# A perceiver block on one core: the batch loop of the second cross-attention written out on five engines

## The chip, the core and the metric

The kernel runs on one core of a Trainium2 chip. The time is in device microseconds (us), for one launch of the whole kernel. The core has five engines, each with an instruction stream of its own: TensorE (PE, with its weight loads shown apart as PEld), VectorE (DVE), ScalarE (ACT), GpSimd (POOL) and SyncE (SP), which here only issues transfers. They meet at semaphores.

## The reference, cut to what matters

The model has two layers. Each is a cross-attention to a context, a self-attention and a feed-forward part, on a state x of 8 x 64 tokens by 512. The change touches the cross-attention of layer 1:

```python
def _L1_xattn_ref(q, kv, key_padding_mask, Wq, bq, Wkv, bkv, Wo, bo):   # q 8x64x512, kv 8x1601x512
    Q = (q @ Wq + bq).reshape(Bc, Tq, H, HD).transpose(0, 2, 1, 3)       # H = 16 heads of HD = 32
    KV = (kv @ Wkv + bkv).reshape(Bc, Tk, 2, H, HD).transpose(2, 0, 3, 1, 4)
    attn = jnp.einsum('bhqd,bhkd->bhqk', Q, KV[0]) * scale
    attn = jnp.where(key_padding_mask[:, None, None, :], -jnp.inf, attn)
    out = jnp.einsum('bhqk,bhkd->bhqd', jax.nn.softmax(attn, axis=-1), KV[1])
    return out.transpose(0, 2, 1, 3).reshape(Bc, Tq, Dm) @ Wo + bo
```

Around it stand layer 0 (cross-attention, self-attention, a routed feed-forward part with 64 experts) before, and layer 1's self-attention and an 8-bit feed-forward product behind.

## The kernel before, in words

The kernel is written engine by engine, with the order of the work on each laid down by hand. The second cross-attention runs over batch elements b = 0 to 7 and, in each, over four units dc = 0 to 3 of four heads (128 feature columns). A unit does the following for its 1601 keys:

- PE turns the exponentials of the unit (L1085, `turn_p`: transposes, four groups tg = 0 to 3), multiplies them with the values (L1102, `pv`: matmuls on 32 columns of the array, the last group of which has 65 rows), and spreads the row sums (L1111, `sums`).
- Between these steps PE makes what the next units need. It is listed in `SLOTS`, a table of short words: "k2" is a key group (L1041, twelve matmuls on chunk 2 of the context), "v5" a value group (L1050, twelve matmuls on tile 5), "s1" the scores of one chunk (L1068, six matmuls). Key and value products use operands split in a rounded part and a rest, hence three matmuls for each of four slices. `SLOTS[0][0]`, with which every batch element opens, is "v0 k0".
- ACT makes the rounded keys `kh` (L1174), copies half of the turned exponentials to `pTx` (L1196), takes the exponentials (L1184), and rounds the context of b + 1 chunk by chunk in unit dc = 2 (L1167, `ctx_high`).
- DVE makes the keys' rest (L1238), adds the bias to the values (L1231), masks and takes maxima (L1249), copies the other half to `pTx`, and scales the result (L1301, L1303).
- POOL takes the next unit's queries (L987 to L992, `take_q`) and subtracts the rounded context from the raw one (L970, `ctx_rest`).
- SP loads the mask (L950) and four chunks of the context of the next batch element (L940, `load_ctx`), each behind a wait on PE's key groups, `kx_made`.

On each engine the batch elements are a hardware loop (`Fori`): PE, ACT and DVE loop over b = 0 to 6 and have b = 7 written out behind the loop; POOL has b = 0 ahead of its loop and loops over 1 to 7; SP has b = 1 ahead and loops over 2 to 7. In a loop b is a register, so every semaphore count that depends on b is worked out by the engine's sequencer, and slices by b are dynamic addresses (`bass.ds`). For PE:

```python
            for w in PRE[1]:
                token(-1, 3, w)
            with pe.Fori(0, B - 1) as b:
                for dc in range(4):
                    unit(b, dc)
            for dc in range(3):
                unit(B - 1, dc)
            unit(B - 1, 3, more=False)
```

PE's buffers of results are two banks of PSUM used in turn (`bank_of`), so PE waits for ACT's and DVE's reading of the group before the last; `kl_ready`, `vx_ready`, `ptx_act`, `ptx_dve` and `lo_ready` are the semaphores by which it would wait for the others.

Of the kernel before, what the change touches and what calls it, by code (L numbers as in the profile page):

```python
# [26 lines left out]
P = 128  # L27
B, S1, D, S2 = 8, 64, 512, 1601
# [25 lines left out]
def perceiver(nc, a, out):  # L54
# [3 lines left out]
    with ExitStack() as ctx:  # L58
        def sb(name, shape, dt=F32):
            return ctx.enter_context(nc.sbuf_tensor(name, shape, dt))  # L60

        def sem(name):
            return ctx.enter_context(nc.semaphore(name))
# [24 lines left out]
        mask8 = sb("mask8", [P, S2], U8)  # L88
# [176 lines left out]
        mask_ld = sem("mask_ld"); mask_set = sem("mask_set"); mask_part = sem("mask_part")  # L265
# [41 lines left out]
        def ln_pool(pool, n):  # L307

            pool.wait_ge(mv_ready, n + 1)
            nc.gpsimd.tensor_tensor(rstd[:, :], rstd[:, :], neg_half[:, :], ALU.pow).then_inc(rstd_ready, 1)  # L310
# [162 lines left out]
        def add_out_bias(pool, n, after):  # L473

            pool.wait_ge(xn_ready, NT * after)
            nc.gpsimd.tensor_tensor(x[:, :, :], x[:, :, :],
                                    bias_r[:, :].unsqueeze(1).to_broadcast([P, NT, D]), ALU.add).then_inc(xb_ready, 1)
# [457 lines left out]
        def xattn_sync(sp):  # L935
            def load_ctx(b, bv):

                for c, (k0, n) in enumerate(KC):
                    sp.wait_ge(kx_made, 4 * (4 * b - 1) + c + 1)
                    sp.dma_start(ctx_raw[c][:, :, 0:n],  # L940
                                 a["ctxT"][bv, :, :, k0:k0 + n].rearrange("e p c k -> (e p) c k")
                                 ).then_inc(ctx_ld[c], 16)

            sp.wait_ge(mask_set, 1)
            sp.dma_start(mask8[:, :], a["mask"][1:2, :].to_broadcast([P, S2])).then_inc(mask_ld, 16)
            load_ctx(1, slice(1, 2))
            with sp.Fori(2, B) as b:
                sp.wait_ge(ld_l1q, 16)
                sp.wait_ge(mask_set, b)
                sp.dma_start(mask8[:, :], a["mask"][bass.ds(b, 1), :].to_broadcast([P, S2])).then_inc(mask_ld, 16)  # L950
                load_ctx(b, bass.ds(b, 1))

            sp.wait_ge(vx_made, KT_N * 2 * B)
            for g in range(4):
                for odd in range(2):
                    r = slice(HD * (2 * odd + g // 2), HD * (2 * odd + g // 2 + 1))
                    sp.dma_start(slot[2][HD * g:HD * g + HD, odd::2, :], a["l1_wo"][r, g % 2::2, :]).then_inc(ld_l1o, 16)
            sp.dma_start(slot[3][:, :, :], a["l1a_wq"]).then_inc(ld_l1a, 16)
            sp.wait_ge(kx_made, 4 * 4 * B)
            sp.dma_start(slot[0][:, :, :], a["l1a_wk"]).then_inc(ld_l1a, 16)  # L960
            sp.dma_start(slot[1][:, :, :], a["l1a_wv"]).then_inc(ld_l1a, 16)
            sp.wait_ge(xb_ready, 3)
            sp.wait_ge(xx_ready, NT)
            sp.dma_start(bias_r[:, :], a["l1a_bo"].to_broadcast([P, D])).then_inc(ld_boa1, 16)
            sp.dma_start(slot[2][:, :, :], a["l1a_wo"]).then_inc(ld_l1ao, 16)
# [10 lines left out]
        def xattn_pool(pool):  # L976

            for v in (ctx_hi[3], ctx_lo[3]):
                nc.gpsimd.tensor_copy(v[:, :, KC[3][1]:], ident[:, P - (KW[3] - KC[3][1]):].unsqueeze(1)
                                      .to_broadcast([P, NC, KW[3] - KC[3][1]])).then_inc(pads_set, 1)  # L980
            nc.gpsimd.memset(qzero[:, :], 0.0).then_inc(pads_set, 1)
            ln_pool(pool, 3)

            def take_q(b, dc, bv):

                hi, lo = qb[dc % 2]
                nc.gpsimd.tensor_copy(qraw[:, :].unsqueeze(1) if not isinstance(bv, int) else qraw[:, :],  # L987
                                      qbd[:, dc, bv, :]).then_inc(q_taken, 1)
                pool.wait_ge(q_taken, 4 * b + dc + 1)
                nc.gpsimd.tensor_tensor(hi[:, :], qraw[:, :], qzero[:, :], ALU.add).then_inc(qh_set, 1)  # L990
                pool.wait_ge(qh_set, 4 * b + dc + 1)
                nc.gpsimd.tensor_tensor(lo[:, :], qraw[:, :], hi[:, :].bitcast(F32),  # L992
                                        ALU.subtract).then_inc(ql_ready, 1)
                pool.wait_ge(ql_ready, 4 * b + dc + 1)

            pool.wait_ge(pads_set, 3)
            pool.wait_ge(q_ready, 3 * NC)
            take_q(0, 0, 0)
            take_q(0, 1, 0)
            pool.wait_ge(ld_bo1, 16)  # L1000
            add_out_bias(pool, 2, 4)
            for dc in (2, 3):
                pool.wait_ge(sx_made, 8 * (dc - 1))
                take_q(0, dc, 0)
            with pool.Fori(1, B) as b:
                pool.wait_ge(q_ready, 3 * NC)
                pool.wait_ge(sx_made, 32 * b - 8)
                take_q(b, 0, bass.ds(b, 1))
                for c in range(4):
                    ctx_rest(b, c)  # L1010
                for dc in (1, 2, 3):
                    pool.wait_ge(sx_made, 32 * b + 8 * (dc - 1))
                    take_q(b, dc, bass.ds(b, 1))

        def xattn_pe(pe):
            def group(b, dc, w):
# [134 lines left out]
            pe.wait_ge(pads_set, 3)  # L1151
            for w in PRE[1]:
                token(-1, 3, w)
            with pe.Fori(0, B - 1) as b:
                for dc in range(4):
                    unit(b, dc)
            for dc in range(3):
# [11 lines left out]
        def xattn_act(act):  # L1169
            def key_high(b, dc, c):  # L1170
                h, n = key_half(b, dc), KN[c]
                act.wait_ge(kx_made, 4 * h + c + 1)
                f = (dc + 1) % 4
                nc.scalar.activation(kh[c % 2][0][:, 0:n], PS[:, bank_of(b, dc, ("k", c)), 0:n], ACT.Identity,  # L1174
                                     bias=bias_c[:, 3, f:f + 1]).then_inc(kh_ready, 1)

            def token(b, dc, w):
                if w[0] == "k":
                    key_high(b, dc, w[1])

            def ex(h, dc, p):
                act.wait_ge(sx_max, 2 * h + p + 1)
                v = sx[2 * (dc % 2) + p][:, 0:S2]
                nc.scalar.activation(v, v, ACT.Exp, scale=SC, bias=nmx[:, p:p + 1],  # L1184
                                     accum_out=rsx[:, p:p + 1]).then_inc(px_ready, 1)

            def unit(b, dc, more=True):
                u = 4 * b + dc
                share = SLOTS[dc] if more else [[]] * 5
                fetch = dc == 2 and not isinstance(b, int)  # L1190
                for w in share[0]:
                    token(b, dc, w)
                for tg in range(4):
                    n, w = (P, 4 * P) if tg < 3 else (rows(KT_N - 1), P)
                    act.wait_ge(ptx_made, 8 * u + 2 * tg + 1)
                    nc.scalar.copy(pTx[0][0:n, :, :].rearrange("p a b -> p (a b)")[:, 0:w],  # L1196
                                   PS[0:n, 2, 0:w]).then_inc(ptx_act, 1)
                    if fetch and tg in (0, 3):
                        ctx_high(b + 1, tg)
                    for w in share[tg + 1]:  # L1200
                        token(b, dc, w)
                    if fetch and tg in (0, 1):
                        ctx_high(b + 1, tg + 1)
                if more:
                    for p in range(2):
                        ex(u + 1, dc + 1, p)

            ctx_high(0, 2)
            ctx_high(0, 3)
            for w in PRE[0]:  # L1210
                token(-1, 3, w)
            xt_copy(act, nc.scalar.copy, 3, (0, 2))
            for w in PRE[1]:
                token(-1, 3, w)
            for p in range(2):
                ex(0, 0, p)
            with act.Fori(0, B - 1) as b:
                for dc in range(4):
                    unit(b, dc)
            for dc in range(3):  # L1220
                unit(B - 1, dc)
            unit(B - 1, 3, more=False)

        def xattn_dve(dve):
# [35 lines left out]
            def token(b, dc, w):  # L1260
                {"k": key_low, "v": v_out, "s": masked}[w[0]](b, dc, w[1])
# [67 lines left out]
            q_dve(dve, 2, 2, bank=0)  # L1329
            for w in PRE[1]:  # L1330
                token(-1, 3, w)
            with dve.Fori(0, B - 1) as b:
                for dc in range(4):
                    unit(b, dc)
            for dc in range(3):
# [445 lines left out]
```

## Time and profile before

| what | value |
|---|---|
| median of 3 runs | 1924.59 us (1922.11 to 1925.12) |
| the profiled execution | 1925.49 us, its span 1923.7 us |
| busy share of PE / DVE / ACT / POOL | 93% / 38% / 24% / 20% |
| mean granted clock of PE over the span | 0.955 |
| loop of the second cross-attention on PE | 894.13 to 1681.27 us |
| instruction packets: q8 / q14 | 101 (1.65 MB) / 45 (0.37 MB) |

The profile is of one execution. Start times in it are counted from the first instruction, and the span ends with the last. "Busy" is the time in which an engine has an instruction running; register, branch and semaphore instructions don't count. A wait named "issue" is one for which the profile shows no other engine as the cause. The granted clock of PE is a share of its full 2.4 GHz; 0.5 is 1.2 GHz.

### The profile page before, as it was taken

The numbers are of one execution on the slowest core, as the hardware profiler recorded it, in microseconds if no ns is written. First come the engines' busy times: TensorE is split into PE (matmuls) and PEld (weight loads), VectorE is DVE, ScalarE is ACT, GpSimd is POOL, SyncE is SP. The second block draws the span as 40 slices with busy tenths as digits, with TensorE's granted clock in tenths as the row PEclk, the third lists the DMA queues.
The fourth block names the chain that finished last, engine by engine and source line by source line (L and its number), as shares of the span: only waits on it lengthen the run. The fifth ranks groups of instructions, "written<-read, shape, count | busy, mean of one in ns | idle before, by whom it ended". The sixth has DMA issues, their size and how long they took to land. (4 is left out here: it accounts for less than half of the span.)

```text
span 1923.7 us, 33205 instructions
## 1 busy us (share of the span) xinstructions
PE 1781.9 (93%) x12620; PEld 1333.7 (69%) x12621; DVE 728.8 (38%) x1853; ACT 463.8 (24%) x720; POOL 383.7 (20%) x430
## 2 busy tenths in 40 slices
PE   8867899999999999969999999999999999998875
PEld 3545565666666666557888888888888888985453
DVE  2544561111111111144444545444444544443364
ACT  1111101222222222212422424232242413322010
POOL 2010004333333333311210303012030301200100
PEclk9788899999999999979999999999999999999987
DMA  7000229999999999820200202010020201002100
GB/s 274 0 1 1 105 86 323 333 333 329 333 335 330 332 334 333 256 86 1 61 16 2 70 7 70 7 51 26 2 70 7 70 7 48 23 1 88 49 1 22
DMA packets 67634, 231.88 MB, mean 121 GB/s; under 512 B 6880, under 2 KB 24544, under 8 KB 57376
## 3 DMA queue, kind: packets, MB, share of 16 engines
q1 hardware_dynamic: 53152, 196.29, 29.4%
q0 software_dynamic: 14336, 33.56, 7.2%
q8 instruction: 101, 1.65, 0.4%
q14 instruction: 45, 0.37, 0.1%
HBM read 208.07 MB, written 21.76 MB: 119 GB/s over the span
## 5 line engine op out<-in xcount | busy, mean ns | idle before, releaser
L1050 PE MATMUL PS<-S_r 128*128 128x256 f32 x2496 | 335.4, 290 | 20.0 <-issue 13.8
L1050 PEld LDWEIGHTS PS<-S_r 128*128 128x128 f32 x2496 | 310.8, 192 | 47.7 <-issue 39.3
L1041 PE MATMUL PS<-S_r 128*128 128x384 f32 (+1 forms) x1536 | 311.1, 352 | 0.0
L1041 PEld LDWEIGHTS PS<-S_r 128*128 128x128 f32 x1536 | 270.1, 190 | 10.8 <-issue 3.0
L1249 DVE CUSTOM_DVE_ANT_0 R<-PS,maskadd 128x384 f32<-128x384 f32 (+1 forms) x256 | 136.3, 570 | 30.3 <-PE PS L1068 27.9
L1587 DVE COPY R<-PS 128x256 f32<-128x256 f32 x64 | 27.2, 425 | 298.8 <-PE PS L1481 256.6
L1196 ACT COPY S<-PS 128x512 f32<-128x512 f32 (+1 forms) x128 | 64.4, 503 | 299.9 <-PE PS L1085 299.9
L987 POOL COPY S<-qbd 128x128 f32 (+1 forms) x32 | 9.4, 293 | 633.7 <-PE PS L1068 610.4
L1231 DVE TENSOR_TENSOR R<-PS,vbias 128x256 f32<-128x256 f32 (+1 forms) x208 | 88.2, 424 | 119.7 <-PE PS L1050 116.1
L970 POOL TENSOR_TENSOR S_r<-S,S_r 128x1536 fp32r<-128x1536 f32 (+2 forms) x32 | 118.4, 3720 | 70.4 <-ACT S_r L1167 70.4
L1492 PE MATMUL PS<-R 128*128 128x512 f32 (+1 forms) x288 | 131.6, 592 | 0.8 <-DVE R L1588 0.8
L1085 PE MATMUL PS<-ident,R 128*128 128x128 f32 (+1 forms) x832 | 117.8, 280 | 4.0 <-ACT R L1184 4.0
L1184 ACT ACTIVATE R<-R,nmx 128x1601 f32<-128x1601 f32 x64 | 104.0, 1628 | 63.0 <-DVE nmx L1257 63.0
L1421 POOL DMA_INDIRECT moe_acc<-x,scol x64 | 103.0, 1609 | 52.1 <-POOL scol L1417 48.3
L1545 ACT ACTIVATE x<-PS,w_tab 128x512 f32<-128x512 f32 x64 | 44.0, 688 | 287.1 <-PE PS L1492 287.1
L1291 DVE COPY S<-PS 128x512 f32<-128x512 f32 (+1 forms) x128 | 75.4, 589 | 74.9 <-PE PS L1085 74.2
L1085 PEld LDWEIGHTS PS<-ident,R 128*128 128x128 f32 (+1 forms) x832 | 90.8, 141 | 14.1 <-ACT R L1184 4.5
L1492 PEld LDWEIGHTS PS<-R 128*128 128x128 f32 (+1 forms) x288 | 54.7, 190 | 56.9 <-issue 45.9
L1238 DVE SCALAR_TENSOR_TENSOR kh0l<-PS,bias_c,kh0h 128x384 fp32r<-128x384 f32 x64 | 39.5, 618 | 133.9 <-ACT kh0h L1174 133.9
L1580 DVE TENSOR_TENSOR R<-R,PS 128x352 f32<-128x352 f32 x64 | 33.3, 521 | 143.8 <-issue 137.8
L1238 DVE SCALAR_TENSOR_TENSOR kh1l<-PS,bias_c,kh1h 128x384 fp32r<-128x384 f32 x64 | 41.7, 652 | 116.3 <-ACT kh1h L1174 116.3
L1470 PE MATMUL PS<-qbd,R 128*128 128x352 f32 x256 | 81.1, 459 | 0.7 <-ACT R L1527 0.7
(254 smaller groups left out, 2399.4 us busy)
## 6 DMA issues: line engine op xcount, KB each, us to landing
R<-in_w_gu SPq DMA_DIRECT2D x34, 1408.0 KB, 19.1
R<-in_w_dna SPq DMA_DIRECT2D x50, 512.0 KB, 17.6
qbd<-in_w_gu SPq DMA_DIRECT2D x16, 1408.0 KB
S<-in_w_gu SPq DMA_DIRECT2D x16, 1408.0 KB
S<-in_ctxT SPq DMA_DIRECT2D x24, 768.0 KB, 4.9
R<-in_w_dnb SPq DMA_DIRECT2D x50, 192.0 KB, 18.0
xnT<-in_w_dna SPq DMA_DIRECT2D x16, 512.0 KB
S<-in_ctxT SPq DMA_DIRECT2D x8, 898.0 KB, 5.0
```

What stands on the lines that cost most here:

```text
L970: nc.gpsimd.tensor_tensor(lo, raw, hi.bitcast(F32), ALU.subtract).then_inc(s, 1)
L1041: last = nc.tensor.matmul(PS[:, bank, 0:n], w3[0][:, cc, f0:f0 + P], x3[i][:, cc, 0:n], start=(cc == 0 and w3 is wkv_hi and x3 is ctx_hi), ...
L1050: last = nc.tensor.matmul(PS[:, bank, 0:256], x3[need][:, cc, k0:k0 + P], w3[1][:, cc, f0:f0 + 256], start=(cc == 0 and w3 is wkv_hi and x ...
L1085: last = nc.tensor.transpose(PS[0:n, 2 + p, i * P:(i + 1) * P], sx[2 * (dc % 2) + p][:, kt * P:kt * P + n], ident[:, :])
L1184: nc.scalar.activation(v, v, ACT.Exp, scale=SC, bias=nmx[:, p:p + 1], accum_out=rsx[:, p:p + 1]).then_inc(px_ready, 1)
L1231: nc.vector.tensor_tensor(vx[hf][0:n, i, :], PS[0:n, bank_of(b, dc, ("v", i)), 0:256], vbias[0:n, hf * 256:hf * 256 + 256], ALU.add).then_ ...
L1238: nc.vector.scalar_tensor_tensor(out=lo[:, 0:n], in0=PS[:, bank_of(b, dc, ("k", c)), 0:n], scalar=bias_c[:, 3, f:f + 1], in1=hi[:, 0:n].bi ...
L1249: nc.vector.tensor_tensor_reduce(out=sx[2 * ((dc + 1) % 2) + p][:, k0:k0 + n], in0=PS[:, p, 0:n], in1=maskadd[:, k0:k0 + n], scale=1.0, sc ...
L1291: nc.vector.tensor_copy(pTx[1][0:n, :, :].rearrange("p a b -> p (a b)")[:, 0:w], PS[0:n, 3, 0:w]).then_inc(ptx_dve, 1)
L1421: pool.indirect_dma_start(out=acc[k % 2], out_offset=bass.IndirectOffsetOnAxis(ap=scol[:, k:k + 1], axis=0), in_=yrow[k], in_offset=None, ...
L1470: last = nc.tensor.matmul(PS[:, gu, 0:I], xgT[k % 2][:, c, :], wgu[k][:, c, gu, :], start=(c == 0), stop=(c == NC - 1))
L1492: last = nc.tensor.matmul(PS[:, 3, :], hT[0:w, j, :], wdn[k][0:w, j, :], start=(j == 0), stop=(j == 2))
```

## The change

The `Fori` loops of the second cross-attention on the five engines become Python loops, so the code of every batch element stands in each engine's stream, one behind the other. The counts of the waits and the slices are then constants. Two conditions that told the loop's body from the rest by the type of b are put in another form and select the same work. The number and order of the computing and transferring instructions is the same on every engine. Each engine has no jump left in this stage: before, PE, ACT and DVE jumped back six times, POOL six times and SP five times. Two other loops, over expert tiles (`Fori` on SP and POOL and their like on the other engines), stay.

```diff
@@ xattn_sync
-            with sp.Fori(2, B) as b:
+            for b in range(2, B):
                 sp.wait_ge(ld_l1q, 16)
                 sp.wait_ge(mask_set, b)
-                sp.dma_start(mask8[:, :], a["mask"][bass.ds(b, 1), :].to_broadcast([P, S2])).then_inc(mask_ld, 16)
-                load_ctx(b, bass.ds(b, 1))
+                sp.dma_start(mask8[:, :], a["mask"][b:b + 1, :].to_broadcast([P, S2])).then_inc(mask_ld, 16)
+                load_ctx(b, slice(b, b + 1))
@@ xattn_pool
-            with pool.Fori(1, B) as b:
+            for b in range(1, B):
...
-                take_q(b, 0, bass.ds(b, 1))
+                take_q(b, 0, b)
...
-                    take_q(b, dc, bass.ds(b, 1))
+                    take_q(b, dc, b)
@@ xattn_pe
-            with pe.Fori(0, B - 1) as b:
+            for b in range(B - 1):
                 for dc in range(4):
                     unit(b, dc)
@@ xattn_act
-                fetch = dc == 2 and not isinstance(b, int)
+                fetch = dc == 2 and b < B - 1
...
-            with act.Fori(0, B - 1) as b:
+            for b in range(B - 1):
@@ xattn_dve
-            with dve.Fori(0, B - 1) as b:
+            for b in range(B - 1):
```

## Rows read from the trace of the kernel before

**Rows 1.** The page: busy time and share of the span.

```profile
PE 1781.9 (93%) x12620; PEld 1333.7 (69%) x12621; DVE 728.8 (38%) x1853; ACT 463.8 (24%) x720; POOL 383.7 (20%) x430
```

**Rows 2.** Windows: stretch, length, busy time of each engine, PE's clock, DMA share, GB/s.

```profile
894.13:1681.27 787.14, 770.99 (x7898) 686.94 (x7897) 367.28 (x1106) 253.31 (x364) 134.99 (x112) 0.99 0.11 33
...
1780.00:1923.70 143.70, 101.26 (x479) 60.08 (x480) 71.13 (x97) 17.27 (x30) 8.41 (x4) 0.81 0.07 24
```

**Rows 3.** All waits of PE from 894.13 to 1681.27: total, times, longest.

```profile
PE PS L1050 <- issue: 13.8, 6, 2.6
PE PS L1102 <- ACT S L1196: 2.4, 7, 0.5
```

**Rows 4.** Timeline of PE at the first jump back: start, length, group [wait].

```profile
999.97 0.32 PE L1102 MATMUL PS<-S,R 65*32 65x64 f32 x8
1002.51 2.38 PE L1050 MATMUL PS<-S_r 128*128 128x256 f32 x12 [2.23 <-issue]
1004.70 3.14 PE L1041 MATMUL PS<-S_r 128*128 128x384 f32 x12
1007.68 1.03 PE L1085 MATMUL PS<-ident,R 128*128 128x128 f32 x8
```

**Rows 5.** Timeline of PE where the seventh pass ends and b = 7 begins.

```profile
1677.40 0.32 PE L1102 MATMUL PS<-S,R 65*32 65x64 f32 x8
1677.65 1.70 PE L1050 MATMUL PS<-S_r 128*128 128x256 f32 x12
1679.18 2.25 PE L1041 MATMUL PS<-S_r 128*128 128x384 f32 x12
1681.27 1.04 PE L1085 MATMUL PS<-ident,R 128*128 128x128 f32 x8
```

**Rows 6.** Windows: L1102 (65x64) to the next L1085 at each pass's end.

```profile
999.97:1007.68 7.71, 5.48 (x34) 5.29 (x33) 1.22 (x4) 2.12 (x4) 0.00 (x0) 0.78 0.03 6
1113.32:1120.82 7.50, 5.46 (x33) 5.27 (x33) 1.22 (x4) 2.12 (x4) 0.00 (x0) 0.77 0.03 7
1226.62:1232.68 6.06, 3.95 (x33) 3.76 (x33) 1.22 (x4) 2.12 (x4) 0.00 (x0) 1.00 0.02 5
1338.27:1346.20 7.93, 5.49 (x33) 5.29 (x33) 1.22 (x4) 2.12 (x4) 0.00 (x0) 0.78 0.03 8
1451.79:1458.04 6.25, 3.92 (x33) 3.73 (x33) 1.22 (x4) 2.12 (x4) 0.00 (x0) 1.00 0.02 5
1563.86:1571.78 7.92, 5.30 (x33) 5.10 (x33) 1.22 (x4) 2.12 (x4) 0.00 (x0) 0.78 0.03 8
1677.40:1681.27 3.87, 3.87 (x34) 3.74 (x34) 1.22 (x4) 2.15 (x4) 0.00 (x0) 1.00 0.01 2
```

**Rows 7.** DMA queues, 1002.6 to 1010: packets, MB, share.

```profile
q8 instruction: 2, 0.03, 2.3%
```

**Rows 8.** Windows of units dc = 0 and 1: of b = 6 and of b = 7.

```profile
1571.78:1627.25 55.47, 55.47 (x565) 49.36 (x564) 25.81 (x77) 15.75 (x25) 2.44 (x6) 1.00 0.02 2
1681.27:1736.74 55.47, 55.47 (x566) 49.36 (x564) 25.54 (x77) 15.74 (x25) 1.22 (x3) 1.00 0.04 12
```

**Rows 9.** DMA queues: first 894.13 to 1681.27, then each stretch of rows 8.

```profile
q8 instruction: 76, 1.25, 0.7%
q14 instruction: 34, 0.28, 0.1%
...
q8 instruction: 4, 0.07, 0.5%
```

**Rows 10.** Timeline of ACT after the first jump and after the fall-through.

```profile
1007.88 0.58 ACT L1174 ACTIVATE kh0h<-PS,bias_c 128x384 fp32r<-128x384 f32 x1 [5.79 <-PE PS L1041]
...
1681.47 0.58 ACT L1174 ACTIVATE kh0h<-PS,bias_c 128x384 fp32r<-128x384 f32 x1 [1.92 <-PE PS L1041]
```

**Rows 11.** Timeline of SP: the context loads of b = 1 and of b = 2.

```profile
947.72 11.47 SPq L940 DMA_DIRECT2D S<-in_ctxT  x4
...
1061.43 11.46 SPq L940 DMA_DIRECT2D S<-in_ctxT  x4
```

## The prediction

> **What bounds the kernel now.** I read the page first, then went stage by stage. TensorE (PE) is busy for 93% of the span and VectorE, the next, for 38% [rows 1]. The page's chain of work that ended last is no help here: it reaches back only to 1780 us, after the loop. So the question is what PE does not do in the second cross-attention. That stage has a clean frame. Each unit opens with the same eight transposes of L1085; the first unit of the loop begins at 894.13 us, and the last batch element (b = 7), which is already written out behind the loop, at 1681.27 us. Between the two lie 787.14 us with PE busy for 770.99 of them [rows 2]. The view of waits says what fills the rest: 13.8 us in six waits put down to "issue", each before a group of L1050, up to 2.6 us long, and 2.4 us in seven short waits for ScalarE (ACT) [rows 3]. 770.99 + 13.8 + 2.4 = 787.2, so nothing else is missing. Nowhere in these 787 us does PE wait for VectorE (DVE), for GpSimd (POOL) or for a transfer.
>
> Six is the number of times a loop of seven passes jumps back. The timeline of PE shows the place. Unit dc = 3 ends with eight matmuls of L1102 of form 65x64, and the next pass opens with a value group of twelve matmuls of L1050, then a key group of twelve of L1041, then the transposes. At 999.97 us the eight start, 0.32 us long; the twelve start at 1002.51, after 2.23 us in which PE waits for nothing that the profile shows. They then take 2.38 us and the key group 3.14, and the transposes begin at 1007.68 [rows 4]. When the seventh pass ends, the same instructions follow, but in line, without a jump: the eight start at 1677.40, the twelve at 1677.65 with no wait, take 1.70 and 2.25 us, and the transposes begin at 1681.27 [rows 5]. The work is the same by the code (SLOTS[0][0] is "v0 k0" for every b) and by the counts in the windows (33 or 34 matmuls recorded). So the trace of before holds its own control: the price of a jump back is the length of this stretch with one, less 3.87 us.
>
> **The change part by part.** *The jumps of PE go.* The stretch from the eight matmuls to the transposes measures 7.71, 7.50, 6.06, 7.93, 6.25 and 7.92 us at the six jumps, and 3.87 at the fall-through [rows 6]. Less 3.87 each, that is 3.84 + 3.63 + 2.19 + 4.06 + 2.38 + 4.05 = 20.15 us. It splits in two: 13.8 us of waiting, and 20.15 - 13.8 = 6.4 us by which the matmuls behind the jump are slower. The slower ones are found at four of the six jumps, where PE is busy for 5.3 to 5.5 us in the stretch instead of 3.9, and there the mean granted clock is 0.77 or 0.78; at the other two it is 1.00 and the busy time 3.92 and 3.95, as in the fall-through [rows 6]. That is: after the idle gap the clock was granted at the lower of its levels (1.2 rather than 2.4 GHz) for a while, four times out of six, at 1.4 to 1.6 us each. With no gap, PE is busy without a break up to the key group, as at 1677, where the clock stayed at 1.00. I take all of it as gained: **-20.2 us**. The least it can be by these rows is the waits alone, -13.8, if the clock dips came from something other than the gap.
>
> What causes the 2.0 to 2.6 us is read from the instruction transfers. Two packets of the instruction queue q8, whose 16 KB blocks fit PE's number of instructions, run between 1002.6 and 1010 us, just behind the jump [rows 7]; the pace over the stretch is one in 787 / 76 = 10 us. The loop stretch has 76 packets of q8 with 1.25 MB [rows 9], some 16 KB each and eleven a pass: the body doesn't stay on the engine, it is brought in anew on every pass. A jump to its top finds nothing there. The Trainium skill ("Runtime: NRT & Kernel Launch", section "Instruction fetch mechanics") says that fetching ahead is purely sequential and that a taken branch to a place outside the small window stalls on the fetch of the target; by that rule all six waits go as well, and the trace agrees with its six waits of 2.0 to 2.6 us.
>
> *Written out, does the stream keep up?* The body of PE was fetched eleven blocks a pass already, so writing it out adds no traffic worth naming. Two units of b = 7, all in line, give the answer: 55.47 us with PE busy for 55.47 [rows 8] and four q8 packets. The same two units in the loop, from 1571.78, take 55.47 us too [rows 8], with four q8 packets as well [rows 9]. So blocks that follow in line cost nothing, and the register values that waits in the loop compare with, constants in b = 7, cost PE nothing either: that edit is worth **0.0 us** (bounds: none seen at 0.01 us in 55; over seven passes, below 0.2 either way).
>
> *ACT, DVE and POOL lose their jumps.* At PE's first jump ACT waits 5.79 us for PE's first key group; at the fall-through, without the gap, it still waits 1.92 us for PE [rows 10]. Their jumps lie under PE's work, so **0**. If that cover went, their own price would be at most the same 2.3 us a jump, and those are removed too, so this term cannot turn against the change. What the gap gave them was time to catch up. The fall-through shows that they don't need it: PE ran from 1681.27 for 55.47 us without a wait.
>
> *SyncE's loop.* It loads a mask and four context chunks for each b, and the four chunk loads hang behind waits on PE's key groups. In the first pass these are loads with a constant address, as they all will be afterwards; in the second the address comes from a register. Four issues span 11.47 us in the first pass and 11.46 in the second [rows 11]. No difference: **0**. Behind the loads stand ACT's rounded copies, then POOL's subtractions, then PE's groups of dc = 3 on the new chunks. PE shows no wait for POOL in any of the seven passes [rows 3], also not in the first, which it entered without a gap. The chain is released by PE's own key groups of dc = 2, later than the jump, so it moves with PE. If a chunk did come late, PE would wait at L1050 or L1041 for POOL, and the constant addresses would still not be its cause. No instruction is added to an engine, none changes its shape, and no new wait is made.
>
> *After the loop.* Everything from 1681 on starts 20.2 us earlier. From 1780 us to the end PE works in bursts and the mean clock is 0.81 [rows 2]. Where the dips fall may change a little; I allow two of them either way at 1.6 us, **0 +/- 3.2**.
>
> Sum: -20.2. The profiled execution took 1925.49 us for a span of 1923.7, so 1.8 us lie around it, and the median of the runs is 1924.59, 0.9 below it. The change comes off the span, so the forecast is 1924.6 - 20.2 = **1904.4 us**, 1.0% faster. The measurement can tell about 0.2% (3.9 us) from no change.
>
> **Rivals.** *1. Only the waits go.* The clock dips near the jumps have another cause, for instance they come due by themselves in a stage this dense. For it: dips came at only four of six jumps. Against it: the loop stage's mean clock is 0.99 [rows 2], and in b = 7 there is none at the same place. It gives 1924.6 - 13.8 = 1910.8 us. Chance 0.05.
>
> *2. The gap isn't the jump's.* Instruction blocks arrive late for some reason in the stream itself, and written-out code meets the same holes elsewhere. Then nothing is gained but the branch instructions: 1924.6 less under 1 us. The nearest evidence against it is rows 8: four blocks in line and no hole. The Trainium skill ("Advanced Engine Details and Errata", section "Control Flow Timing") gives about 108 ns for a compare-and-branch; by that figure alone six jumps would be 0.6 us, an estimate, and the change would be worth nothing. The rows at the jumps, 2.0 us and more, say otherwise. Chance 0.03.
>
> *3. Slower: the other engines starve.* ACT, DVE, POOL and SyncE bring their code over q14, 34 packets in the loop stretch [rows 9]. If in one long stream these came late, each exposed one would cost what PE's gap does, 13.8 / 6 = 2.3 us, since PE hangs on ACT and DVE within a unit for kh, kl and pTx. From 9 exposed of 34 on (9 x 2.3 = 20.7) it outweighs the gain; with half of them exposed, 17 x 2.3 - 20.2 = +18.9 us, 1943.5. Against it: in b = 7 these engines run in line and PE waits for none of them over 55 us. Chance 0.03.
>
> The forecast itself has 0.89. So faster by over 0.2%: 0.89 + 0.05 = 0.94; within 0.2%: 0.03; slower: 0.03. The range is the likeliest's own: 3.2 us for the clock on either side and about 1 for the median (the three runs spread from 1922.11 to 1925.12, more of it downward), which makes 1900 to 1908.6; I stretch the top to 1909.5, towards rival 1.
>
> **What the profile after would show.** PE's six waits before L1050 put down to "issue" are gone in the stage, and the twelve value matmuls start 0.25 us after the eight of L1102 at every b, as at 1677.65. The first jump lies between transposes at 894.13 and 1007.68 us, a pass of 113.55; the pass from 1571.78 to 1681.27, which ends in the fall-through, is 109.49 us. All seven should be 109.5 to 109.7 (113.55 - 3.84). The stretch from the first unit to b = 7 shrinks from 787.14 to 767.0 us. The instruction bytes of q8 stay near 1.65 MB. I would be wrong if PE showed "issue" waits of about 2 us at other places, if PE began to wait for kh, kl or pTx at more than the seven short places, or if the clock in the stage fell below 0.99.

## The result: 1902.8 us, and the profile after

The changed kernel took 1902.83 us in the median of five runs (1899.86 to 1904.58), the kernel before 1924.59 beside it. The ratio is 0.9888, with a 95% interval from 0.9873 to 0.9904. The forecast was 1904.4, in a range from 1900.0 to 1909.5.

The profiled span is 1900.6 us. PE's stretch from the first transposes of b = 0 to those of b = 7, which was 787.14 us [rows 2], is here, in the view of windows (stretch, length, busy time of PE, PEld, DVE, ACT, POOL, PE's clock, DMA share, GB/s):

```profile
891.46:1658.30 766.84, 764.72 (x7898) 681.04 (x7896) 364.94 (x1106) 253.24 (x364) 134.74 (x112) 1.00 0.11 33
...
1658.30:1713.77 55.47, 55.47 (x565) 49.36 (x564) 25.55 (x77) 15.72 (x25) 1.21 (x3) 1.00 0.05 12
...
1758.00:1900.60 142.60, 101.20 (x479) 60.10 (x480) 70.53 (x97) 17.25 (x30) 8.41 (x4) 0.81 0.06 23
```

It is 20.30 us shorter with the same 7898 matmul records, and two written-out units of b = 7 last the same 55.47 us as before [rows 8]. All waits of PE in the stretch (total, times, longest), against [rows 3]:

```profile
PE PS L1102 <- ACT S L1196: 2.1, 7, 0.5
```

The six waits of 13.8 us are gone and nothing came in their place. The timeline of PE where b = 1 begins, against [rows 4]:

```profile
997.16 0.32 PE L1102 MATMUL PS<-S,R 65*32 65x64 f32 x8
997.41 1.68 PE L1050 MATMUL PS<-S_r 128*128 128x256 f32 x12
998.93 2.28 PE L1041 MATMUL PS<-S_r 128*128 128x384 f32 x12
1001.05 1.03 PE L1085 MATMUL PS<-ident,R 128*128 128x128 f32 x8
```

It is 3.89 us from the eight matmuls to the transposes instead of 7.71; the fall-through before had 3.87. The instruction queues on the page, 101 and 45 packets before:

```profile
q8 instruction: 88, 1.44, 0.3%
q14 instruction: 26, 0.21, 0.0%
```

The other 2.8 us of the span's 23.1 are not the change's. The first transposes come 2.67 us earlier (894.13 to 891.46), and nothing ahead of them was changed. Over all runs below they come between 888.85 and 894.46 us, and kernels that keep PE's loop are found at both ends; so comparisons here go by the stretch, which leaves that scatter out. From the end of the stretch to the end of the span it is 242.3 us, and 242.4 before.

### The profile page after: what moved, and what is told of

The parts are those of the page before. It is cut to its first block and busy times, and to the rows that moved or that the text cites. A ratio compares the mean times of both kernels' runs of the same rounds, so it can differ in the third digit from the quotient of the medians.

```text
span 1900.6 us, 31650 instructions
## 1 busy us (share of the span) xinstructions
PE 1773.1 (93%) x12620; PEld 1325.8 (70%) x12621; DVE 726.5 (38%) x1853; ACT 463.4 (24%) x720; POOL 383.0 (20%) x430
## 3 DMA queue, kind: packets, MB, share of 16 engines
q8 instruction: 88, 1.44, 0.3%
## 5 line engine op out<-in xcount | busy, mean ns | idle before, releaser
L1050 PE MATMUL PS<-S_r 128*128 128x256 f32 x2496 | 331.2, 287 | 6.2 <-DVE kh0l L1238 6.2
L1050 PEld LDWEIGHTS PS<-S_r 128*128 128x128 f32 x2496 | 306.9, 190 | 33.5 <-issue 24.6
L1041 PEld LDWEIGHTS PS<-S_r 128*128 128x128 f32 x1536 | 267.8, 189 | 10.9 <-issue 3.0
L987 POOL COPY S<-qbd 128x128 f32<-128x128 f32 x32 | 9.3, 292 | 614.3 <-PE PS L1068 590.9
L1085 PE MATMUL PS<-ident,R 128*128 128x128 f32 (+1 forms) x832 | 118.0, 280 | 3.8 <-ACT R L1184 3.8
L1085 PEld LDWEIGHTS PS<-ident,R 128*128 128x128 f32 (+1 forms) x832 | 90.9, 141 | 14.0 <-ACT R L1184 4.4
```

What stands on the lines that cost most here:

```text
L1041: last = nc.tensor.matmul(PS[:, bank, 0:n], w3[0][:, cc, f0:f0 + P], x3[i][:, cc, 0:n], start=(cc == 0 and w3 is wkv_hi and x3 is ctx_hi), ...
L1050: last = nc.tensor.matmul(PS[:, bank, 0:256], x3[need][:, cc, k0:k0 + P], w3[1][:, cc, f0:f0 + 256], start=(cc == 0 and w3 is wkv_hi and x ...
L1085: last = nc.tensor.transpose(PS[0:n, 2 + p, i * P:(i + 1) * P], sx[2 * (dc % 2) + p][:, kt * P:kt * P + n], ident[:, :])
```

## The experiments

They are made in the second cross-attention, and the stretch named above is the measure; each stretch is that of one profiled execution. "Issue" waits are PE's in it.

**One part at a time: PE alone.** The kernel before, with one loop of the five written out:

```diff
-            with pe.Fori(0, B - 1) as b:
+            for b in range(B - 1):
```

> PE alone is written out, the other four engines keep their loops. Measured on PE from the first transposes of b = 0 to those of b = 7 (787.14 us before, 766.84 after). Theory (PE's own jumps are the whole cost): 766.5 to 767.5 us, and a time of 1902 to 1906 us. Rival (a part of the gain came from the jumps of ACT, DVE, POOL or SP, or from constant addresses on SP): 768 us or more, with new waits of PE for ACT or DVE behind their jumps.

Measured: 766.65 us in the stretch, no issue wait, 1901.87 us in the median, ratio 0.9876 (0.9858 to 0.9894). The time lies 0.1 us below what was expected. PE's loop is the whole of it, and the other four engines can keep theirs: PE's waits for ACT are 1.9 us in all, against 2.1 in the changed kernel.

**The other four.** The changed kernel, with PE's `Fori` put back:

> The converse: ACT, DVE, POOL and SP are written out, PE keeps its loop. Theory: the six waits of 2.0 to 2.6 us before L1050 stay, the stretch is 786 to 788.5 us, the time 1922 to 1926 us. Rival (the engines share the cost, so that each part alone gives some of it): clearly under 785 us.

Measured: ratio 0.9995 (0.9985 to 1.0005), no change. Waits and window:

```profile
PE PS L1050 <- issue: 13.7, 6, 2.6
PE PS L1102 <- ACT S L1196: 2.8, 7, 0.6
```
```profile
893.78:1684.03 790.25, 773.76 (x7897) 689.74 (x7896) 364.82 (x1106) 253.26 (x364) 134.82 (x112) 0.99 0.10 32
```

The issue waits are those of before to 0.1 us. The stretch is 3.1 us longer than in the kernel before, outside what was expected. Of that, 2.8 us are PE's busy time, 773.76 against 770.99, and the rest is waiting for ACT. The clock was low behind five of the six jumps in this execution, and behind the second for longer: that one took 9.26 us from the eight matmuls to the transposes, where the longest before took 7.93. PE's stream is the same in both kernels. So the clock's part of the price differs from one execution to the next (6.3 us of busy time before, 9.0 here, over the 764.72 of the written-out kernel), and the waits' part hardly does.

**Two jumps instead of six.** The changed kernel with

```diff
-            for b in range(B - 1):
-                for dc in range(4):
-                    unit(b, dc)
+            with pe.Fori(0, B - 2, 2) as b:
+                for step in range(2):
+                    for dc in range(4):
+                        unit(b + step, dc)
+            for dc in range(4):
+                unit(B - 2, dc)
```

> As the changed kernel, but PE loops over pairs of batch elements (three passes, b = 6 and 7 written out): two jumps back instead of six, each over a body twice as long. Theory (a price per jump back, 2.2 to 4.1 us each by the six of before, 3.4 on average): 766.84 + 2 x 3.4 = 773.6 us, from 771.2 to 775.0; time about 1909.6 us; two waits put down to issue. Rival (a price per batch element or per loop as such, for example of register values in the waits): 780 us or more. Rival (the price grows with the length of the body jumped over): waits of 4 us and more each.

Measured: 774.02 us, 1911.74 us in the median (1906.84 to 1915.72), ratio 0.9921 (0.9897 to 0.9945). The waits:

```profile
PE PS L1050 <- issue: 5.1, 2, 2.6
PE PS L1102 <- ACT S L1199: 2.6, 7, 0.8
```

There are two waits of 2.5 and 2.6 us, and the stretch is 7.2 us longer than written out, or 3.6 a jump. The price goes by the jump, not by the batch element, and a body of twice the length costs no more.

**Six jumps over nothing.** The changed kernel, still written out, with

```diff
             for b in range(B - 1):
+                if b:
+                    with pe.Fori(0, 2) as again:
+                        pe.wait_ge(w_lo, 2)
                 for dc in range(4):
```

> The changed kernel, written out, with six jumps back on PE put in again at the same six places (ahead of b = 1 to 6), but each over a body of one instruction only: a loop of two passes round a wait that is long fulfilled. It adds nothing else. Theory (the price is the bringing in of code that has left the engine, not the jump): under 0.5 us for each, 766.8 to 769.8 us in the stretch, no wait of 2 us. Rival (every jump back throws away what was brought in ahead, near or far): six waits of 2 us and more, 779 to 787 us, time 1915 to 1923 us.

Measured: 767.06 us, ratio 0.9884 (0.9867 to 0.99), no issue wait. The stretch is 0.22 us longer than in the changed kernel, and two executions with the same written-out stream on PE differ by 0.19 (766.84 and 766.65), so no cost of these six jumps can be told from none. The branch as such is not what was paid for.

**How long a body may be.** The changed kernel with added loops of plain matmuls ahead of b = 1 to 6, of N passes:

```diff
+                if b:
+                    pe.wait_ge(zx_ready, 4 * b + 1)
+                    with pe.Fori(0, N) as again:
+                        for _ in range((30, 120, 240, 480, 900, 1300)[b - 1]):
+                            nc.tensor.matmul(PS[0:HD, 4, 256:256 + S1], ident[:, 0:HD], same_q[:, :],
+                                             start=True, stop=True)
```

> The changed kernel with added work on PE, which no output depends on: ahead of b = 1 to 6 stands a loop of two passes over a body of 30, 120, 240, 480, 900 and 1300 small matmuls (128x32 by 64, each a weight load and a matmul, so 60 to 2600 instructions), so one jump back for each size. Theory (code that is still on the engine costs nothing to jump to): no wait inside the loop of 60 instructions, one of 2 us or more at 2600; the sizes between tell how much stays. Rival (distance doesn't matter beyond the shortest): a wait of like size from 240 instructions on. Rival (any real body is free, and the 2.3 us of the batch loop have to do with its waits on registers): no wait at any size.

> As the run before it with four passes, so three jumps back for each size. Theory: the same waits by size, three at each size that has one there; three times the total. Rival (the first jump back brings the body in and later ones find it): one wait at each size, as with two passes.

Each of the two ran once, for its trace (2608.27 and 3315.38 us with the added work). The sizes named there are half the true ones. The trace shows 12280 of these matmuls for 6140 written ones: each runs as two matmuls, each with its own weight load, so the bodies have 120, 480, 960, 1920, 3600 and 5200 instructions. The waits, first with two passes, then with four:

```profile
PE PS L1159 <- issue: 8.4, 3, 2.9
```
```profile
PE PS L1159 <- issue: 22.7, 9, 2.7
```

Three waits with one jump at each size, nine with three. The timeline of PE with two passes shows which sizes. The rows are the body of 240 written matmuls (both passes merged into one row, 960 in the trace) and the start of the second pass of each of the three larger:

```profile
1253.58 53.76 PE L1159 MATMUL PS<-same_q,ident 128*32 128x64 f32 x960 [0.74 <-DVE xnT L1309]
...
1474.16 55.43 PE L1159 MATMUL PS<-same_q,ident 128*32 128x64 f32 x960 [2.90 <-issue]
...
1743.34 66.86 PE L1159 MATMUL PS<-same_q,ident 128*32 128x64 f32 x1165 [2.89 <-issue]
...
2103.90 36.31 PE L1159 MATMUL PS<-same_q,ident 128*32 128x64 f32 x647 [2.64 <-issue]
```

At 960 instructions, and at 120 and 480, there is no wait at the jump. At 1920, 3600 and 5200 there are 2.90, 2.89 and 2.64 us. The price is a step, not a slope. That puts aside both rivals of the two-pass run: 480 and 960 instructions are free, and large bodies without any wait on a register are not. It is paid at each jump, which puts aside the rival of the four-pass run. The step lies somewhere from 960 to 1920 instructions; where was not tried. A pass of the batch loop has 7898 / 7 = 1128 matmuls, with the weight loads over 2250 instructions, beyond the step.

The instruction queue agrees. From two passes to four q8 grows from 184 packets to 280, by 96. The three large bodies run twice more, 2 x (960 + 1800 + 2600) x 2 = 21440 instructions. In the changed kernel's stretch 62 packets with 1.02 MB carry 7898 matmuls and 7896 weight loads, so some 64 bytes an instruction and 256 instructions a packet. That makes 84 packets, and 12 are left for six more jumps, two for each. None is left for the small bodies, which were not brought in again.

The traces also time these transfers. In the kernel before, the wait behind the first jump ends at 1002.51 us [rows 4]. The view of DMA queues from 990 to 1000.3 us has one q8 packet, which starts at 999.76, and the next starts only at 1002.98:

```profile
q8 instruction: 1, 0.02, 0.6%
```

In all eight kernels here that have such waits, those of the next section included, each of the 56 has a q8 packet that starts 2.4 to 3.1 us before the wait ends. By this timing PE stands still for one block of code on its way.

**Hiding the fetch.** With four engines written out and PE in its loop, the loop is turned by two groups, so that the jump has 24 long matmuls ahead of it:

```diff
+            for w in SLOTS[0][0]:
+                token(0, 0, w)
             with pe.Fori(0, B - 1) as b:
                 for dc in range(4):
-                    unit(b, dc)
+                    unit(b, dc, opened=dc == 0)
+                for w in SLOTS[0][0]:
+                    token(b + 1, 0, w)
```

(`opened` leaves out the two groups at the head of the unit.)

> PE keeps its loop (the other engines are written out), but the loop is turned by two groups: the 'v0 k0' that opens a batch element is made at the end of the pass before, so that the jump comes behind twelve value and twelve key matmuls (3.9 us of work without a wait on a late engine) instead of behind the eight short matmuls of L1102, which have just waited for ptx_act and ptx_dve. Same work, same order on PE, six jumps back. Theory (the price is a fetch of 2.3 us and more, of which PE's sequencer can hide as much as it is ahead of the array): the wait before the transposes is under 1 us or gone, 767 to 775 us in the stretch, time 1903 to 1911 us. Rival (the fetch starts only when all that stands before the jump is done, so no cover helps): waits of 2.0 to 2.6 us remain, 782 to 790 us.

Measured: the contrary of what was expected, and of what the rival said too. 1943.18 us, ratio 1.0099 (1.0083 to 1.0116), slower than before; 805.84 us in the stretch, twelve issue waits of 22.2 us. The timeline of PE at the first jump:

```profile
996.57 2.24 PE L1041 MATMUL PS<-S_r 128*128 128x384 f32 x12
999.95 0.43 PE L1085 MATMUL PS<-ident,R 128*128 128x128 f32 x2 [1.14 <-issue]
1002.99 1.44 PE L1085 MATMUL PS<-ident,R 128*128 128x128 f32 x6 [2.60 <-issue]
```

The first wait did shrink, to between 0.65 and 1.14 us at the six jumps, from 2.0 to 2.6. But after two matmuls comes a second, of 2.5 to 3.05 us. The page has 107 q8 packets, six more than the 101 of the kernel before: three extra blocks a jump and not two. The new theory: code comes in blocks of 256 instructions, and the top of the turned loop happens to lie a few instructions ahead of a block's end. PE gets the block, uses up its last few instructions, and stands again for the next. In the kernel before, the same end lies some 56 instructions behind the top, behind nearly 4 us of matmuls, and the second fetch is done under them.

The 56 is reckoned from the code and the two matmuls, not read from a trace. The theory can be tested by moving code by a few instructions and changing nothing else in the stretch. Ahead of each kind of loop go n small matmuls, four instructions each:

```diff
             for w in PRE[1]:
                 token(-1, 3, w)
+            pe.wait_ge(zx_ready, 1)
+            for _ in range(n):
+                nc.tensor.matmul(PS[0:HD, 4, 256:256 + S1], ident[:, 0:HD], same_q[:, :], start=True, stop=True)
```

The plain loop with n = 12:

> The kernel with PE's loop and the other four engines written out (790.25 us in the stretch), with twelve small added matmuls on PE ahead of the loop, run once (some 1 us, outside the stretch; no output depends on them). Their 48 instructions, a weight load and a matmul for each of two parts, move the loop's top and all behind it by 48 places. Theory (code comes in blocks of 256 instructions; in the turned loop the second wait after two transposes marks a block's end, which lies some 56 instructions behind the top of the untouched loop; moved by 48 it lies some 8 behind it): two waits at every jump, 2.0 to 2.6 us ahead of L1050 and another of 2 to 3 us after a few of its matmuls, 797 to 808 us in the stretch, time 1930 to 1946 us. Rival (the second wait of the turned loop comes from its instructions, the waits on px_ready and registers, not from its place): one wait a jump as without the added matmuls, 787 to 791 us.

Measured: 806.80 us, 1947.36 in the median, ratio 1.0124 (1.0107 to 1.0142). Timeline at the first jump, then the waits:

```profile
1000.05 0.32 PE L1102 MATMUL PS<-S,R 65*32 65x64 f32 x8
1002.89 0.50 PE L1050 MATMUL PS<-S_r 128*128 128x256 f32 x2 [2.52 <-issue]
1005.90 2.29 PE L1050 MATMUL PS<-S_r 128*128 128x256 f32 x10 [2.51 <-issue]
```
```profile
PE PS L1050 <- issue: 27.8, 12, 2.6
PE PS L1102 <- ACT S L1199: 1.7, 7, 0.2
```

The turned loop with n = 8:

> The turned loop (805.84 us in the stretch, two waits a jump) with eight small added matmuls, 32 instructions, ahead of the loop. Theory: the loop's top now lies just behind a block's start, so the second wait (2.5 to 3.05 us) is gone and the first, of 0.65 to 1.14 us, part of which the 24 matmuls ahead of the jump hide, stays: 771 to 780 us in the stretch, time 1906 to 1916 us. Rival: two waits as before, 803 us or more.

Measured: 774.04 us, 1913.33 in the median, ratio 0.9947 (0.993 to 0.9964). Timeline at the first jump, the waits, and the window:

```profile
1001.79 2.24 PE L1041 MATMUL PS<-S_r 128*128 128x384 f32 x12
1004.94 1.09 PE L1085 MATMUL PS<-ident,R 128*128 128x128 f32 x8 [0.90 <-issue]
```
```profile
PE PS L1085 <- issue: 6.3, 6, 1.3
PE PS L1102 <- ACT S L1203: 1.7, 7, 0.2
```
```profile
894.39:1668.43 774.04, 765.98 (x7897) 680.64 (x7896) 365.21 (x1106) 253.70 (x364) 134.79 (x112) 1.00 0.11 33
```

Both stretches came out as the theory says (the plain loop's time is 1.4 us above the range expected): 48 instructions made a second wait where there was none, at the third matmul, and 32 took it away. The q8 packets went to 107 and to 101. The same loop over the same work costs 7.2, 23.4, 39.0 or 40.0 us more than written out, by how often it jumps, where it begins in the code and what stands ahead of its jump.

No version beat the written-out one. PE's loop alone written out (0.9876) and all five (0.9888) can't be told apart.

## Why the prediction was right

- *The jumps of PE, -20.2 us.* Right in place and size: the stretch lost 20.30 us against 20.15 forecast. The price was read off the fall-through inside the same trace. That the two agree to 1% is owed to setting the result against the very execution that the price was read from: the medians differ by 21.8 us, and the other execution with the same loop on PE, in the converse run, is 23.4 us longer than written out. So the nearness to 1% is in part luck. The seven passes came out at 109.48 to 109.77 us, against 109.5 to 109.7.
- *The split into 13.8 of waiting and 6.4 of slower matmuls.* Right. PE's busy time in the stretch fell from 770.99 to 764.72, by 6.3, and the mean clock went from 0.99 to 1.00. Rival 1, by which the clock's part would have stayed, is refuted: without the gaps the matmuls behind them ran at full speed at all six places.
- *A body brought in anew on every pass.* Right in its core: long bodies pay, short ones don't, and the step lies under the body's length. But two readings were wrong. The two packets of [rows 7] start after the wait has ended at 1002.51; the one PE stood for starts at 999.76. And the eleven blocks a pass are not all body. Nine are (62 packets in the stretch after, 62 / 7 = 8.9), and two a jump were extra. So the forecast that the bytes of q8 stay near 1.65 MB was wrong: they fell to 1.44. No term of the sum hung on it. Two a jump is not the whole difference either: the loop over pairs has 95 packets on its page against 88, seven more for two jumps, and what the other three carry no run shows.
- *ACT, DVE, POOL and SP at 0.* Right, shown by writing them out alone (0.9995) and by leaving them in their loops while PE has none (766.65 us in the stretch).
- *Constants in place of registers at 0.* Right as far as PE shows it; 767 us are accounted for by busy time and ACT's seven short waits.
- *After the loop, 0 +/- 3.2.* Right: from b = 7's first transposes to the end it is 242.3 us against 242.4, and late in it the mean clock is 0.81 both times.
- *Rival 2, holes in the stream itself, and rival 3, starving engines.* Neither came. q14 carried fewer packets, 26 instead of 45, and PE's waits for ACT are the same seven. Rival 2 drew on the Trainium skill ("Advanced Engine Details and Errata", section "Control Flow Timing") for about 108 ns a compare-and-branch. The six near jumps lengthened PE's stretch by at most 0.22 us together; what they cost PE's sequencer under its other work no run shows.
- What the prediction did not see is how narrow its case was: had the loop stood 48 instructions further on in the kernel before, the same change would have been worth about 40 us in the stretch instead of 20, an estimate from the plain loop with n = 12 (806.80 against 766.84).

## What to carry to other kernels

Where an engine that bounds the kernel runs a loop, look in its timeline at the first instructions behind each jump back: a wait named "issue" there is the price of the jump, with whatever the matmuls behind it lose at a lower clock, and the pass behind which no jump follows is the control. Short bodies (up to 960 instructions on PE here) jump for nothing; for long ones, write out the loop of the bounding engine alone, since the others' cost no time here. Where that isn't possible, put long work without waits ahead of the jump, and check for a second wait shortly behind it, which a few instructions ahead of the loop move away.

## What the runs showed of the hardware that was not expected

- A jump back on TensorE costs nothing visible over a body of up to 960 instructions and 2.4 to 2.9 us over one of 1920, 3600 or 5200, whatever the length. The Trainium skill ("Runtime: NRT & Kernel Launch", section "Instruction fetch mechanics") gives PE room for 2048 instructions. The trace agrees at 960, 3600 and 5200; the body of 1920 would fit by that figure and was not free, so the measured step, between 960 and 1920, is the one to go by. Whether it was the blocks at its two ends and those fetched ahead that pushed the 1920 out was not tried. The same section's rule for a taken branch, on which the prediction drew, speaks of a window of two pages, 512 instructions; by it the body of 960 should have stalled, and it did not.
- Where the loop's top lies in the code decides whether PE stands once or twice at a jump: 23.4 us for six jumps in the one case and 40.0 in the other, with 48 instructions between them. That the place counts within a 16 KB block fits both moves that were tried; the blocks' bounds themselves are in no trace.
- The granted clock followed the gaps. With six waits of up to 1.3 us the mean over the stretch stayed at 1.00, and behind single waits of 2.0 to 2.6 us it was low at some jumps and not at others (mean 0.99). With two waits a jump, 22.2 us in all in the turned loop and 27.8 in the plain one, the mean was 0.97, and PE's busy time was 16.5 and 12.5 us over the 764.72 of the written-out kernel, 42% and 31% of what was lost there.
